# GpSimd instead of ScalarE makes the 16-bit high parts of normalised queries and keys, for four of eight pairs of heads

## The reference

```
x = rmsnorm(tokens) ; q = x @ Wq ; k, v = split(x @ Wkv)         # 16 heads of 64
q = q / |q| * (q_gamma + 1) * 8 ; k = k / |k| * (k_gamma + 1) * 8 # per head
sim = tanh(q @ k.T / 50) * 50 / 8
out = softmax(sim) @ v ; return out @ Wo
```

## Time and profile before

| | |
|---|---|
| median of 3 runs | 1099.09 us (1098.5 to 1099.18) |
| the profiled execution | 1098.77 us, its span 1096.6 us |
| TensorE busy | 1048.1 us (96%) |
| ScalarE busy | 1033.9 us (94%) |
| VectorE busy | 928.6 us (85%) |
| GpSimd busy | 852.4 us (78%) |
| chain that ended last | PE 42%, ACT 38%, waiting for nothing that is shown 11% |

### The profile page before, as it was taken

How to read it: one execution, slowest core, us unless ns; L and a number is a source line. 1 busy time by engine, 2 the same in 40 slices (tenths; PEclk the granted TensorE clock), 3 DMA queues, 4 the chain that set the end, 5 groups by cost and what they waited for, 6 DMA issues and landing times.

```text
span 1096.6 us, 33887 instructions
## 1 busy us (share of the span) xinstructions
PE 1048.1 (96%) x12889; PEld 842.7 (77%) x12889; DVE 928.6 (85%) x2185; ACT 1033.9 (94%) x1545; POOL 852.4 (78%) x784
## 2 busy tenths in 40 slices
PE   5789999999999999999999999999999999999987
PEld 4467787777787777787777788777787777787776
DVE  6988889888889888889888889888889888889872
ACT  4699999999999999999999999999999999999996
POOL 7677878887878887878887878887878887878763
PEclk9899999999999999999999999999999999999999
DMA  3344444344454334444334444434444334344341
GB/s 114 65 72 81 74 85 80 71 78 84 74 84 80 74 77 82 75 85 79 75 75 84 75 84 80 72 77 84 76 83 79 78 71 84 76 82 80 65 92 31
DMA packets 310487, 85.41 MB, mean 78 GB/s; under 512 B 282020, under 2 KB 309816, under 8 KB 310328
## 3 DMA queue, kind: packets, MB, share of 16 engines
q1 hardware_dynamic: 310328, 83.25, 39.8%
HBM read 11.09 MB, written 4.19 MB: 14 GB/s over the span
## 4 chain that ended last, share of the span: by engine, by line
PE 42%; ACT 38%; issue 11%; SPq 2%; DVE 2%; POOL 2%; DMA 2%; ACTq 0%; POOLq 0%
ACT clamped L597 11%; PE ps_scores L511 10%; ACT probs L604 9%; PE ps_aux L486 5%; PE ps_aux L431 4%; PE ps_y L559 4%; ACT L641 4%; ACT halves L612 4%; ACT L604 4%; PE ps_o L537 3%; PE ps_aux L433 3%; PE ps_aux L432 3%; ACT hid L641 3%; PE ps_o L539 2%; PE ps_o L538 2%
## 5 line engine op out<-in xcount | busy, mean ns | idle before, releaser
L973 POOL TENSOR_TENSOR probs_lo<-probs 128x1024 f16<-128x1024 f32 x256 | 485.1, 1895 | 208.1 <-ACT probs L604 208.1
L597 ACT ACTIVATE clamped<-ps_scores 128x1024 f32<-128x1024 f32 x256 | 265.9, 1039 | 24.9 <-PE ps_scores L511 20.9
L604 ACT ACTIVATE probs<-clamped 128x1024 f32<-128x1024 f32 x256 | 273.0, 1066 | 2.6
L763 DVE TENSOR_TENSOR halves<-ps_n,halves 128x512 f16<-128x512 f32 x256 | 174.9, 683 | 65.9 <-ACT halves L612 65.8
L537 PEld LDWEIGHTS ps_o<-v_hi,probs 128*128 128x128 bf16 x2048 | 183.9, 98 | 60.9 <-issue 58.4
L511 PE MATMUL ps_scores<-heads_T 64*128 64x256 f16 x3072 | 212.2, 271 | 11.8 <-ACT clamped L597 6.1
L537 PE MATMUL ps_o<-v_hi,probs 128*128 128x65 bf16 x2048 | 213.8, 195 | 5.5 <-POOL probs_lo L973 1.4
L538 PE MATMUL ps_o<-v_lo,probs 128*128 128x64 bf16 x2048 | 211.7, 193 | 0.0
L539 PE MATMUL ps_o<-v_hi,probs_lo 128*128 128x65 bf16 x2048 | 211.3, 194 | 0.0
L431 PE MATMUL ps_aux<-w_hi,xhT_hi 128*128 128x512 f32 x384 | 178.9, 466 | 19.3 <-ACT qk L628 6.8
L538 PEld LDWEIGHTS ps_o<-v_lo,probs 128*128 128x128 bf16 x2048 | 187.3, 98 | 0.0
(11 more groups left out here) (83 smaller groups left out, 1910.8 us busy)
## 6 DMA issues: line engine op xcount, KB each, us to landing
heads_T<-halves SPq DMA_TRANSPOSE x512, 2.5
x_in<-in_L_attn_tokens_dram SPq DMA_DIRECT2D x32, 128.0 KB, 2.4
x_res<-in_L_attn_tokens_dram SPq DMA_DIRECT2D x32, 128.0 KB, 2.3
out_dram<-y_sb SPq DMA_DIRECT2D x32, 128.0 KB, 2.0
sel_raw<-xn SPq DMA_DIRECT2D x192, 4.0 KB
qk<-in_L_attn_Wkv_dram SPq DMA_DIRECT2D x2, 512.0 KB, 5.6
qk<-in_L_attn_Wq_dram SPq DMA_DIRECT2D x1, 512.0 KB, 3.6
qk<-in_L_ffn_W_dram SPq DMA_DIRECT2D x2, 256.0 KB
```

The costliest lines, as they stand in the source:

```text
L597: nc.scalar.activation(clamped[:].rearrange("p j n -> p (j n)"), ps_scores[:].rearrange("p j n -> p (j n)"), ACT.Tanh).then_inc(clamp_done, 1)
L604: nc.scalar.activation(probs[:, pair % RING].rearrange("p j n -> p (j n)"), clamped[:].rearrange("p j n -> p (j n)"), ACT.Exp, bias=LIFT, ...
L973: g.tensor_tensor(probs_lo[:, buf].rearrange("p j n -> p (j n)"), probs[:, buf].rearrange("p j n -> p (j n)"), probs[:, buf].rearrange("p ...
```

## The change

ScalarE keeps the cast for pairs 2 to 5. For pairs 0, 1, 6 and 7 GpSimd makes the high half itself, as a product of `qk` and the reciprocal roots, written as f16 (`hi_part`). VectorE still writes `ps_n` for all pairs, and still subtracts. As GpSimd doesn't read PSUM, VectorE copies the 64 roots to SBUF after the last newton step (`root_copy`). GpSimd's pairs have a semaphore of their own; a helper picks the one to wait for. VectorE's `halves` now also waits for its own `normalise`, and the tasks that overwrite `qk` wait for GpSimd too.

```diff
-    [("half", 3), ("tanh",), ("oT", 3, -1), ("exp",), ("half", 4), ("hid", 0, 0), ("hid", 1, 0)],
+    [("tanh",), ("oT", 3, -1), ("exp",), ("hid", 0, 0), ("hid", 1, 0)],
     [("tanh",), ("q", 0, 2), ("exp",)],
-    [("half", 3), ("tanh",), ("q", 1, 2), ("exp",), ("v", 0, 1), ("v", 1, 1)],
-    [("half", 3), ("tanh",), ("exp",), ("k", 0, 2), ("k", 1, 2), ("v", 2, 1)],
+    [("tanh",), ("q", 1, 2), ("exp",), ("v", 0, 1), ("v", 1, 1)],
+    [("tanh",), ("exp",), ("k", 0, 2), ("k", 1, 2), ("v", 2, 1)],
...
-    [("divide",), ("newton", 5), ("newton", 6), ("newton", 7), ("newton", 8), ("normalise",), ("norm_stats",),
+    [("divide",), ("newton", 5), ("newton", 6), ("newton", 7), ("newton", 8), ("root_copy",), ("normalise",), ("norm_stats",),
      ("q", 0, 2)],
...
 POOL_STEPS = [
-    [("lo",)],
+    [("hi", 6, 0), ("lo",)],
     [("square", 2, 1), ("square", 3, 1), ("lo",)],
-    [("bias",), ("lo",)],
+    [("bias",), ("hi", 7, 0), ("lo",)],
     [("select",), ("lo",)],
-    [("lo",)],
+    [("hi", 0, 1), ("hi", 1, 1), ("lo",)],
...
+            def root_copy(st):
+
+                b, _, _ = st.batch(1)
+                dve.wait_ge(newton_step, 9 * b + 9)
+                wait(dve, half_hi_pool, len(GPSIMD_PAIRS) * b)
+                v.tensor_copy(rnorm_sb[:], rnorm).then_inc(rnorm_copied, 1)
...
-                dve.wait_ge(half_hi_made, PAIRS * b + pair + 1)
+                wait_half_hi(dve, b, pair)
+                dve.wait_ge(qk_normed, PAIRS * b + pair + 1)
...
+            def hi_part(st, pair, ahead):
+
+                b, par, _ = st.batch(ahead)
+                if pair == 0:
+                    pool.wait_ge(q_scaled, 4 * b + 4)
+                    pool.wait_ge(k_copied, 4 * b + 4)
+                pool.wait_ge(rnorm_copied, b + 1)
+                wait(pool, heads_turned[pair % 4], 32 * ((PAIRS * b + pair) // 4))
+                r = rnorm_sb[:].rearrange("p (a h) -> p a h", h=HEADS)[:, :, 2 * pair:2 * pair + 2]
+                g.tensor_tensor(halves16[:, pair % 4, 0].rearrange("p a (h d) -> p a h d", d=DH),
+                                pair_of_qk(par, pair).rearrange("p a (h d) -> p a h d", d=DH),
+                                r.unsqueeze(3).to_broadcast([P, 2 * TT, 2, DH]), ALU.mult).then_inc(half_hi_pool, 1)
```

More of the change, by code:

```diff
@@ L105 @@
 NORMALISE_LEAD = 4
+GPSIMD_PAIRS = (0, 1, 6, 7)
+SCALAR_PAIRS = (2, 3, 4, 5)
 SELECT_SLOT = 0
@@ L214, in block_kernel @@
         newton_r = sb("newton_r", [P, TT * 2 * HEADS])
+        rnorm_sb = sb("rnorm_sb", [P, TT * 2 * HEADS])
         at = 4 * (DH + 1)
@@ L288, in block_kernel @@
         half_hi_made = sem("half_hi_made")
+        half_hi_pool = sem("half_hi_pool")
+        rnorm_copied = sem("rnorm_copied")
         half_lo_made = sem("half_lo_made")
@@ L346, in ahead_of, with wait_half_hi @@
             return (ahead, pair) if STAGE[ahead] in st.stages else None
+        def wait_half_hi(eng, b, pair):
+            if pair in GPSIMD_PAIRS:
+                eng.wait_ge(half_hi_pool, len(GPSIMD_PAIRS) * b + GPSIMD_PAIRS.index(pair) + 1)
+            else:
+                eng.wait_ge(half_hi_made, len(SCALAR_PAIRS) * b + SCALAR_PAIRS.index(pair) + 1)
         def run_all(eng, run):
@@ L393, in turn_heads @@
                 wait(sp, scores_done, 2 * PAIRS * (b - 1) + 2 * pair + 2)
-                for half, made in enumerate((half_hi_made, half_lo_made)):
-                    sp.wait_ge(made, PAIRS * b + pair + 1)
+                for half in range(2):
+                    if half == 0:
+                        wait_half_hi(sp, b, pair)
+                    else:
+                        sp.wait_ge(half_lo_made, PAIRS * b + pair + 1)
                     sp.dma_start(heads_T[:, half, pair].rearrange("p t j n -> p (t j) n"),
@@ L626, in aux @@
                         wait(act, qk_normed, PAIRS * (b - 1))
+                        wait(act, half_hi_pool, len(GPSIMD_PAIRS) * (b - 1))
                     t, c = k // 2, 2 + k % 2
@@ L797, in aux @@
                         wait(dve, qk_normed, PAIRS * (b - 1))
+                        wait(dve, half_hi_pool, len(GPSIMD_PAIRS) * (b - 1))
                     t, c = k // 2, k % 2
@@ L863, in run @@
                                 newton(st, *k)
+                        elif what == "root_copy":
+                            if "front" in st.stages:
+                                root_copy(st)
                         elif what == "norm_stats":
@@ L991, in run @@
                                 lo_part(st, s)
+                        elif what == "hi":
+                            if STAGE[k[1]] in st.stages:
+                                hi_part(st, *k)
                         elif what == "square":
```

## The result

The changed kernel takes 1064.87 us, median of 4 runs (1063.81 to 1069.78), against 1098.8 before: a ratio of 0.970, 95% interval 0.9674 to 0.9726. The forecast was 1064. The profiled execution is the slowest of the four, 1069.78 with a span of 1067.6.

What follows compares the result with a forecast made beforehand. ScalarE's path was taken as the bound, TensorE waiting 1.38 us a turn; a ring through GpSimd would leave 1.12 won. 30 turns plus the ends give 35.3 off, 1063.8, so 1064 us; range 1059 to 1069.

Steps and rivals of the forecast that it cites:

- ScalarE's path: ScalarE's gapless work from slot 3's tanh to slot 6, said to make TensorE wait 1.38 us a turn.
- slots 5 and 6: Steps of a turn making those head pairs' scores; TensorE's starts there forecast at 3.95 and 4.98 us, from 4.13 and 6.18.
- the ring: Wait chain, slot 3 scores, lo(4), GpSimd squares, VectorE sums, k projection, next slot 3 scores: forecast to bind at 31.74 us.
- Their 0.94: Casts of pairs 0 and 1 in slots 5 and 6, estimated at 0.46 and 0.48 us of ScalarE's path.
- The multiplications at 1.04 us: GpSimd's four added 128x512 products a turn, taken at the time of its square of the same shape.
- The spare time ahead of lo(4): GpSimd's products for pairs 0 and 1 were to fit before lo(4) with 0.4 us to spare, up to 1.2 each.
- lo(4): GpSimd's low half of the probabilities of slot 4, forecast to start only 0.60 us earlier.
- The sum: Whole kernel: 30 turns x 1.12 us plus the last turns, less 0.4 at the start, together 35.3 won.
- (a): Rival, in the loop: squares arrive in time, TensorE packed, turn 31.48 us, time 1056; chance 15%.
- (b): Rival: GpSimd the bound, still faster, multiplications between 1.23 and 1.5 us; at 1.35, time 1079; chance 22%.
- (c): Rival: GpSimd so slow that it loses, multiplications from 1.50 us on; 1109 at 1.6, 1146 at 1.89; chance 8%.
- (d): Rival: ScalarE's casts were hidden, another wait takes their place, turn stays 32.86 us; chance 4%.

Runs made afterwards that it cites:

- e9: Changed kernel with only the second of VectorE's two sums of squares of k moved, to slot 0 behind normalise: 1056.51 us.
- e11: e9 with SyncE loading the selected rows in slot 1 instead of slot 0, behind the transposes of pair 3: 1055.71 us.
- e12: Changed kernel with pair 6's cast given back to ScalarE, in slot 3 ahead of tanh: 1064.2 us.
- e2: Changed kernel with GpSimd making the high half of pair 7 alone, ScalarE those of the other seven: 1079.58 us.
- e3: Changed kernel with GpSimd making the high halves of pairs 0 and 1 alone, ScalarE those of 2 to 7: 1082.35 us.
- e5: Changed kernel with GpSimd's four multiplications writing only the first of each 64 columns, all waits kept: 1062.74 us.
- e10: Changed kernel with GpSimd's two squares of slot 7 moved to slot 6, ahead of its low half there: 1056.23 us.
- e1: The changed kernel again, no edit, for a second profile: 1065.56 us.
- e4: Changed kernel with both of VectorE's sums of squares of k moved from the end of slot 7 to slot 0, behind the q scaling: 1080.72 us.
- e6: Changed kernel with the multiplications of pairs 6 and 7 made twice, first into a buffer nobody reads: 1093.24 us.

## Why the prediction was right

- **ScalarE's path was the bound, by 1.38 us a turn.** Measured: slots 5 and 6 are shorter by 0.16 and 1.19 to 1.20. With the ring cut (e9 to e11) the turn is 31.48 to 31.49, so 1.37 was there to win. The starts gave it; TensorE's busy time would have given 0.52.
- **The casts are worth what they cover.** Pair 6 nothing (e12), pair 7 its 0.60 (e2: 0.61), pairs 0 and 1 at most what the ring leaves them (e3: 0.52). Their 0.94 was never seen whole: with the ring cut, 1.37 less pair 7's 0.61 is 0.76, and there TensorE is the bound.
- **The multiplications at 1.04 us.** 1051 ns over 128, the least 1041 and the most 1059; nothing of a slowdown by VectorE.
- **The spare time ahead of lo(4) was overstated.** Forecast 0.4 us, measured 0.21 (the idle before lo(4) above). The copy starts at 509.45 and takes 0.22, and GpSimd starts 0.23 after its end; I had let it start at once. By that these multiplications would have begun to delay lo(4) at about 1.15 us each, not at 1.2: an estimate, 1.05 and half of 0.21.
- **The ring at 31.74.** 31.75; e2, e3, e5, e9 and e10 show that it is this ring and not GpSimd's load.
- **The sum.** Forecast 35.3 less; the medians differ by 33.9. In e1's profile, against before: the turns 2 to 29 give 31.5 (28 x 1.12 = 31.4; both profiles have three late turns), turn 30 gives 30.04 - 28.78 = 1.3 (forecast 1.5), the rest from the scores of turn 31 on gives 39.21 - 38.73 = 0.5 (0.6). Up to turn 1 e1 gains 2.2 (before 39.89 + 32.93 + 33.52 = 106.34; e1 104.12), in the first profile it loses 2.2 (108.50). The forecast had 2 x 1.12 - 0.4 = 1.8 for this stretch. With the copy in the kernel turn 2 starts anywhere from 102.8 to 108.5 in the thirteen profiles, and the forecast gave no range for that. So the turn was foreseen, but that the total came within 1 us was in part luck.
- **Not foreseen: one late transpose costs twice.** The forecast asked when pair 2's transposes leave the buffer of pair 6, and in the loop GpSimd indeed never waits for them. It left the same question out for pair 7, which needs pair 3's transposes to be gone. For these GpSimd now waits in some turns, with its whole queue behind that wait. Over the first profile's whole span (5.7 of it once, in the start-up), and in its turn 12:

```profile
POOL halves L1006 <- DMA heads_T<-halves: 15.7, 10, 5.7
```
```profile
438.22 1.05 POOL L1006 TENSOR_TENSOR halves<-qk,rnorm_sb 128x512 f16<-128x512 f32 x1 [1.50 <-DMA heads_T<-halves]
```

  That turn's slot 2 was 0.20 longer, as late turns were before, and slot 0 of the next one 4.28 for 3.83, since the squares came later still. Before the change such a turn cost 0.23 to 0.42 and nothing after it. I had taken the median landing, 2.5 us, for every one: in the first profile landings take up to 5.0. It isn't scatter alone. In that profile GpSimd waits 0.8 to 1.7 in each of the turns 4, 8, 12 and so on to 28, and outside them, from turn 1 on, only in turns 5 (0.7) and 10 (0.1). All late slots 2 in the profiles but one are in those turns. Why every fourth turn stays open.

Of the rivals, (a), packed TensorE, became true only when the ring was cut. (b) and (c) needed a multiplication over 1.2 us. (d) is refuted by the turn of 31.75, and by e2, where one cast alone gives 0.61.

## What to carry to other kernels

When work is taken from the engine that holds the path, look at what that path also brings forward: here only one cast of 0.60 stood ahead of GpSimd's lo(4), while TensorE could win 1.38, and everything behind lo(4) became late by the rest. Follow each engine's order from there back to the bound engine, add the starts up, and compare the ring with the packed work. Here that gave the turn to 0.01 us. An engine 97% full need not be the bound (e5). A task moved "behind" another may have been filling a wait (e4).

## What the runs showed of the hardware

- TensorE's matmuls of 512 f32 columns step by 0.43 us at a granted clock of 0.50 and by 0.23 at 1.00. In one execution they stepped by 0.43 until 28 us, in another of the same kernel until 16; the two differ by 2.5 us at the first scores. None of these profiles has a record of the clock before its first change of pace, so up to there only the steps tell it.
- GpSimd multiplies 128x512 f32 by a broadcast operand into f16 in 1051 ns, 9 ns more than its square without broadcast in f32 (1042).
- Slot 6 of turn 9 takes 5.24 to 5.27 us for 4.98 in seven of the profiles, in the others not. The delay starts on ScalarE: its tanh of slot 5 stands behind 0.37 us of idle where it is 0.09 in other turns, though it follows ScalarE's own exp and the scores are there. The same idle shows in turn 9 of e6 and in turn 5 of e3. In e10:

```profile
345.05 1.03 ACT L612 ACTIVATE clamped<-ps_scores 128x1024 f32<-128x1024 f32 x1 [0.37 <-ACT probs L619]
```

  I have no cause for it. Where the ring binds, as in the first profile and e1, slot 0 of turn 10 is shorter by about as much.
